# Splitting w2 for the experts: eight of them one per tile, in the order of the tile table

## What is computed

```python
    scores = jnp.einsum('bhqd,bhkd->bhqk', qh, kh) / np.sqrt(HD)
    attn = jax.nn.softmax(jnp.where(causal, scores, -jnp.inf), axis=-1)
    out = jnp.einsum('bhqk,bhkd->bhqd', attn, vh)
...
    topw, topi = jax.lax.top_k(probs, K)              # K = 4 of E = 16
    combine = jnp.sum(jax.nn.one_hot(topi, E) * topw[..., None], axis=2)
    def body(acc, expert):
        w1e, b1e, w2e, b2e, ce = expert
        hmid = jax.nn.gelu(x @ w1e + b1e, approximate=False)
        return (acc + (hmid @ w2e + b2e) * ce[:, None], None)
```

## Time and profile before

| | us |
|---|---|
| median of 3 runs | 1704.41 (1701.32 to 1704.91) |
| the profiled execution | 1689.59 |
| its span, from its first to its last instruction | 1687.9 |
| PE busy | 1591.6 (94%) |
| DVE busy | 1191.6 (71%) |
| ACT busy | 1067.2 (63%) |
| POOL busy | 510.5 (30%) |

### The profile page before, as it was taken

How to read it: one execution, slowest core, us unless ns; L and a number is a source line. 1 busy time by engine, 2 the same in 40 slices (tenths; PEclk the granted TensorE clock), 3 DMA queues, 4 the chain that set the end, 5 groups by cost and what they waited for, 6 DMA issues and landing times.

```text
span 1687.9 us, 35758 instructions
## 1 busy us (share of the span) xinstructions
PE 1591.6 (94%) x12470; PEld 1338.8 (79%) x12470; DVE 1191.6 (71%) x2754; ACT 1067.2 (63%) x2702; POOL 510.5 (30%) x430
## 2 busy tenths in 40 slices
PE   5999989999999999999999999997999999999995
PEld 4888866777677777777776776776989999999995
DVE  6988947667776777677677767678775666666662
ACT  4555547666666765676666667667755666666663
POOL 3434400000210300301202103004485555554654
PEclk9999989999999999999999999999999999999998
DMA  3122110000110100200201102045699777777773
GB/s 99 38 88 76 38 63 2 1 26 2 43 50 1 60 33 1 82 11 15 78 1 47 46 2 85 8 155 183 152 245 257 190 173 167 187 169 172 183 159 38
DMA packets 94976, 144.54 MB, mean 86 GB/s; under 512 B 12576, under 2 KB 55120, under 8 KB 94800
## 3 DMA queue, kind: packets, MB, share of 16 engines
q1 hardware_dynamic: 64448, 102.19, 19.3%
q0 software_dynamic: 28896, 38.62, 12.2%
q10 hardware_dynamic: 1456, 1.44, 0.3%
HBM read 90.76 MB, written 51.46 MB: 84 GB/s over the span
## 4 chain that ended last, share of the span: by engine, by line
PE 55%; ACT 16%; DVE 9%; issue 3%; DMA 2%; SPq 1%; POOL 0%; POOLq 0%; DVEq 0%; ACTq 0%
PE ex_H L1753 12%; PE ex_Y L1767 11%; ACT xa_prob L1336 8%; PE xa_work L1251 6%; PE xa_work L1176 6%; PE xa_S L1205 5%; PE xa_work L1187 4%; PE xa_work L1234 4%; PE xa_work L1222 4%; ACT xa_probT L1350 4%; DVE xa_nmax L1454 3%; PE ex_X L1735 2%; DVE xa_prob L1466 2%; DMA out<-ex_y,ahead_bits 1%; DVE xa_q1lo L1447 1%
## 5 line engine op out<-in xcount | busy, mean ns | idle before, releaser
L1336 ACT ACTIVATE xa_prob<-xa_S,xa_nmax 128x512 f32<-128x512 f32 (+3 forms) x512 | 265.9, 534 | 126.8 <-DVE xa_nmax L1454 126.1
L1869 POOL DMA_INDIRECT out<-ex_y,ahead_bits x158 | 259.0, 1640 | 220.0 <-POOLq L1865 92.0
L1753 PE MATMUL ex_H<-ex_xT,ex_w 128*128 128x256 f32 x1896 | 248.3, 288 | 0.1
L1767 PE MATMUL ex_Y<-experts_w_hi,ex_hT 128*128 x1264 | 238.9, 282 | 5.9 <-issue 5.9
L1753 PEld LDWEIGHTS ex_H<-ex_xT,ex_w 128*128 128x128 f32 x1896 | 234.1, 193 | 0.4 <-issue 0.3
L1767 PEld LDWEIGHTS ex_Y<-experts_w_hi,ex_hT 128*128 128x128 f32 x1264 | 200.7, 190 | 6.1 <-issue 6.1
L1454 DVE TENSOR_REDUCE xa_nmax<-xa_S 128x2 f32<-128x1024 f32 (+3 forms) x256 | 198.0, 816 | 1.2 <-PE xa_S L1210 1.2
L1622 POOL DMA_INDIRECT expert_rows<-kept_xn,kept_rows x112 | 112.4, 1004 | 274.1 <-DVE xa_prob L1466 249.3
L1350 ACT ACTIVATE xa_probT<-xa_work 128x512 f32<-128x512 f32 x256 | 139.6, 602 | 80.6 <-PE xa_work L1222 80.6
L1840 DVE TENSOR_TENSOR ex_hT<-ex_h,ex_hT 128x512 fp32r<-128x512 f32 x158 | 109.2, 693 | 107.0 <-ACT ex_hT L1792 103.3
L1767 PE MATMUL ex_Y<-experts_w_lo,ex_hT 128*128 x632 | 177.5, 281 | 0.0
(11 more groups left out here) (363 smaller groups left out, 3614.7 us busy)
## 6 DMA issues: line engine op xcount, KB each, us to landing
ex_w_raw<-in_w SPq DMA_DIRECT2D x29, 512.0 KB, 3.7
kept_x<-expert_rows SPq DMA_DIRECT2D x50, 273.0 KB, 4.5
ahead_ctx<-in_w SPq DMA_DIRECT2D x25, 512.0 KB
ahead_x<-in_w SPq DMA_DIRECT2D x25, 512.0 KB
kept_xn<-expert_rows SPq DMA_DIRECT2D x29, 273.0 KB, 4.6
experts_w_lo<-in_w SPq DMA_DIRECT2D x6, 1024.0 KB, 5.8
expert_rows<-ahead_spare SPq DMA_DIRECT2D x32, 136.5 KB
a_x<-in_x SPq DMA_DIRECT2D x8, 512.0 KB, 4.6
```

The lines of the kernel that those rows point to most:

```text
L1336: m = act.activation(prob[n % 2][:, odd, PROB_AT[i]:PROB_AT[i] + width], SB[slot[at]][:, odd, col:col + width], ACT.Exp, bias=nmax[n % 2][ ...
L1753: m = pe.matmul(bank[:, (f % 2) * ROWS:(f % 2 + 1) * ROWS], ww[:, c, f * P:(f + 1) * P], xx[:, c, :], start=(i == 0), stop=(i == len(terms ...
L1767: m = pe.matmul(bank[:, a * D:(a + 1) * D], hh[:, f, a * P:(a + 1) * P], W2[:, bass.ds(own * WE + f * D, D)], start=(i == 0), stop=(i == l ...
L1869: pool.indirect_dma_start(out, bass.IndirectOffsetOnAxis(tail[j % NT][:, a, 0:1].bitcast(I32), 0), y[j % NY][:, a, :], None, compute_op=AL ...
```

## The change

The eight experts 0, 1 and 8 to 13 are no longer split in a fixed order before tile 0's results. DVE sorts them (`order_w2`, in pair 56): those that own a tile in the first part of the table, by their number, then the others. `high_late` and `low_late` split the first of them behind the last pair and one more in each of tiles 0 to 6, at an address that ACT and DVE load from this order. `results` of tile j waits for the j-th alone (the last for all later tiles). Expert 6's halving moves ahead of the turns of pair 63.

The last batch's chain, the pads, its scatters, the store of its x2, the second part of the table and the four buffers all come three tiles later; the first part of the table holds for 27 tiles. `give_tables` comes right behind `turn_tables`, ahead of `hidden`, and both use the bank of tile 17.

In pairs 57, 59, 61 and in those with p = 4 or 7 of batches 0 to 6, turn 2 comes ahead of `soften` of block 3 in the plan, which changes ACT's order alone.

```diff
-SURE_TILES = 24
+SURE_TILES = 27
+LATE_W2, N_LATE = ((0, (0, 2)), (2, (8, 6))), 8
...
+    def order_w2(self, dve, w, done, late_w2):
+        tiles, rank, ranked = self.scr[0:1, 1, :], self.scr[0:1, 3, 0:N_LATE], self.scr[0:1, 3, N_LATE:2 * N_LATE]
+        for at, (first, n) in LATE_W2:
+            i = dve.tensor_scalar(rank[:, at:at + n], tiles[:, first:first + n], 1.0, float(2 * E), ALU.is_ge, ALU.mult)
+        i.then_inc(done.of("has"), 1)
+        w.wait_ge(done, "has")
+        dve.tensor_tensor(rank, rank, late_w2, op=ALU.subtract).then_inc(done.of("rank"), 1)
+        w.wait_ge(done, "rank")
+        dve.max(ranked, rank).then_inc(done.of("ranked"), 1)
+        w.wait_ge(done, "ranked")
+        dve.tensor_scalar(rank, ranked, float(E), float(2 * E), ALU.is_ge, ALU.mult).then_inc(done.of("had"), 1)
+        w.wait_ge(done, "had")
+        dve.tensor_tensor(self.scr_i[0:1, 0:N_LATE], rank, ranked, op=ALU.subtract).then_inc(done.of("order"), 1)
...
-TURN_AT, W2_IN_PAIR = 14, {61: (2, 3), 62: (4, 5), 63: (14, 15)}
-CHAIN = {1: [("find3", B - 1)], 2: [("norm3", B - 1)], ...
+LATE_MAX = (57, 59, 61)
+TURN_AT, W2_IN_PAIR = 17, {61: (2, 3), 62: (4, 5), 63: (14, 15)}
+CHAIN = {4: [("find3", B - 1)], 5: [("norm3", B - 1)], ...
...
-            plan += [*turns, *high_w2(6, 7), *low_w2(6, 7), *finish, *scatters]
+            plan += [*high_w2(6), *turns, *low_w2(6), *high_w2(7), *low_w2(7), *finish, *scatters]
...
+        in_front = 3 if n in LATE_MAX or coming < B and p in (4, 7) else 2
-        plan += [("scores", (n, 3)), ("scores", (n, 2)), *start, *turns[0:2], *high_w2(*one), ("soften", (n, 3)), *turns[2:4], ("soften", (n, 2))]
+        plan += [("scores", (n, 3)), ("scores", (n, 2)), *start, *turns[0:2], *high_w2(*one), *turns[2:in_front], ("soften", (n, 3)), *turns[in_front:4], ("soften", (n, 2))]
...
-    plan += [("add_b2", (b - 1, 1)), ("store_x2", b - 1), ("split_w1", 0), ("turn_x", 0), ("load_x", 2), *high_w2(8, 1, 0, 9), *low_w2(8, 1),
+    plan += [("add_b2", (b - 1, 1)), ("store_x2", b - 1), ("split_w1", 0), ("turn_x", 0), ("load_x", 2), ("high_late", 0), ("low_late", 0),
...
-        steps = [("turn_x", j + 1), ("load_x", j + 3), ("turn_tables", None), *(high_w2(10, 11, 12, 13) + low_w2(0, 9, 10) if j == 0 else []),
-                 ("hidden", j), *(low_w2(11, 12, 13) if j == 0 else []), *chain[:1], ("split_w1", j + 2), ("load_w1", j + 4), ("results", j - 1), *chain[1:]]
+        steps = [("turn_x", j + 1), ("load_x", j + 3), ("turn_tables", None), ("give_tables", None), ("hidden", j), ("high_late", j + 1), *chain[:1], ("split_w1", j + 2), ("load_w1", j + 4), ("low_late", j + 1), ("results", j - 1), *chain[1:]]
...
+            elif step == "high_late":
+                w.wait_ge(t_dve, "order")
+                w.wait_ge(s_pe, (B * PAIRS - 1, 1, 1))
+                w.wait_ge(pv_pe, (B * PAIRS - 1, 1))
+                for i, loaded in enumerate(w2_in):
+                    w.wait_ge(loaded, i)
+                mine = act.value_load(tables.scr_i[0:1, at:at + 1], min_val=0, max_val=E - 1)
+                act.activation(W2_hi[:, bass.ds(mine * WE, WE)], f32(W2_lo[:, bass.ds(mine * WE, WE)]), ACT.Copy
+                               ).then_inc(high_late.of(at), 1)
...
+            elif step == "low_late":
+                w.wait_ge(high_late, at)
+                mine = dve.value_load(tables.scr_i[0:1, at:at + 1], min_val=0, max_val=E - 1)
+                own = bass.ds(mine * WE, WE)
+                dve.tensor_tensor(W2_lo[:, own], f32(W2_lo[:, own]), f32(W2_hi[:, own]), op=ALU.subtract).then_inc(low_late.of(at), 1)
...
-FEW, MORE, MORE_AT = 2, 4, 20
-CHAIN_AT, CHAIN_END = 3, 12
+FEW, MORE, MORE_AT = 2, 4, 23
+CHAIN_AT, CHAIN_END = 6, 15
...
-                w.wait_ge(gone["low_w2"], 13)
+                w.wait_ge(gone["low_w2"], 7)
+                w.wait_ge(gone["low_late"], min(j, N_LATE - 1))
```

More of the change, by code:

```diff
@@ L144, in of_part @@
     def of_part(part):
-        return ["one", "up", "tiles_i", "tiles", *(("less",) if part else ()), "cum", "hit", "owner", "hit_tiles", "before",
+        return ["one", "up", "tiles_i", "tiles", *(("less",) if part else ()), "cum", *(() if part else ("has", "rank", "ranked", "had", "order")), "hit", "owner", "hit_tiles", "before",
                 *(("some", "first", "behind", "here", "used", "owner_some") if part else ()), "row",
@@ L170, in find_owners @@
         mult, add, sub = ALU.mult, ALU.add, ALU.subtract
-        w.wait_ge(done, "cum")
+        w.wait_ge(done, "cum" if part else "order")
         dve.tensor_scalar(hit, cum, number[:], None, ALU.is_le).then_inc(done.of("hit"), 1)
@@ L916 @@
 OF_LOAD = {e_: i for i, (first, last) in enumerate(LOAD_W2) for e_ in range(first, last)}
-TURN_AT, W2_IN_PAIR = 14, {61: (2, 3), 62: (4, 5), 63: (14, 15)}
-CHAIN = {1: [("find3", B - 1)], 2: [("norm3", B - 1)], 3: [("transpose_x3", (B - 1, c)) for c in range(KC)], 4: [("route", B - 1)],
-         5: [("choose", B - 1)], 6: [("mark", B - 1), ("weigh_gates", B - 1)], 7: [("place", B - 1)], 8: [("turn_gates", B - 1)],
-         9: [("add_b2", (B - 1, 0))], 10: [("add_b2", (B - 1, 1))]}
+LATE_MAX = (57, 59, 61)
+TURN_AT, W2_IN_PAIR = 17, {61: (2, 3), 62: (4, 5), 63: (14, 15)}
+CHAIN = {4: [("find3", B - 1)], 5: [("norm3", B - 1)], 6: [("transpose_x3", (B - 1, c)) for c in range(KC)], 7: [("route", B - 1)],
+         8: [("choose", B - 1)], 9: [("mark", B - 1), ("weigh_gates", B - 1)], 10: [("place", B - 1)], 11: [("turn_gates", B - 1)],
+         12: [("add_b2", (B - 1, 0))], 13: [("add_b2", (B - 1, 1))]}
 ALONE = [at for steps in CHAIN.values() for at in steps if at[0] in ("transpose_x3", "route", "place", "turn_gates", "add_b2")]
@@ L1033, in cross_attention @@
         tables = Tables(sb, lg)
-        sb("room_in_front_of_w2", [P, 16])
+        late_w2 = sb("room_in_front_of_w2", [P, 16])[0:1, 0:N_LATE]
         heads = ExitStack()
@@ L1087, in cross_attention @@
         low_w2 = signal("low_w2", [at for step, at in plan if step == "low_w2"])
+        high_late, low_late = signal("high_late", range(N_LATE)), signal("low_late", range(N_LATE))
         x3_pe, x3_ev = signal("x3_pe", blocks), signal("x3_ev", blocks)
@@ L1378, in scalar @@
                 end = B * PAIRS - 1
-                w.wait_ge(s_pe, (end, 1, 1), at == 0)
-                w.wait_ge(s_pe, (end - 1, 1, 1), at == 1)
                 w.wait_ge(pv_pe, (end - PAIRS // 2, 1), at in (2, 3))
-                w.wait_ge(pv_pe, (end - 1, 1), at in (6, 7, 8))
-                w.wait_ge(pv_pe, (end, 1), 9 <= at < 14)
+                w.wait_ge(pv_pe, (end - 1, 1), at in (6, 7))
                 w.wait_ge(k_pe, end, at >= 14)
@@ L1584, in vector @@
                     tables.count_tiles(dve, w, t_dve, 0, kept, count)
+                    w.wait_ge(late_set, 0)
+                    tables.order_w2(dve, w, t_dve, late_w2)
                 elif at == 1:
@@ L1595, in gpsimd @@
                 pool.memset(f32(gates[:]), 0.0).then_inc(gates_zero.of(0), 1)
+                for to, (first, n) in LATE_W2:
+                    i = pool.iota(late_w2[:, to:to + n], [[1, n]], base=first, channel_multiplier=0, allow_small_or_imprecise_dtypes=True)
+                i.then_inc(late_set.of(0), 1)
             elif step in ("find2", "find3"):
@@ L1723, in tensor @@
                 w.wait_ge(x_lo, TURN_AT)
-                tables.transpose(pe, w, t_dve, XB[0], ident).then_inc(tables_pe.of(0), 1)
+                tables.transpose(pe, w, t_dve, x_bank(TURN_AT), ident).then_inc(tables_pe.of(0), 1)
             elif step == "turn_x":
@@ L1813, in vector @@
                 w.wait_ge(tables_pe, 0)
-                tables.give_out(dve, t_dve, 1, XB[0], ahead, routing)
+                tables.give_out(dve, t_dve, 1, x_bank(TURN_AT), ahead, routing)
             elif step == "split_w1":
```

14 lines of the change are left out of this document (7 added, 7 removed).

## The result

| | before | after |
|---|---|---|
| median of 5 runs each, us | 1704.41 (1701.32 to 1706.37) | 1689.28 (1686.68 to 1693.37) |
| ratio to before, 95% interval | | 0.9918 (0.9897 to 0.9939) |
| the profiled execution / its span, us | 1689.59 / 1687.9 | 1687.96 / 1686.2 |

A forecast was written before the change was run, and what follows sets the result against it. PE was taken to bound the kernel, so only its stalls and half-clock stretches could give time. Gains 9.6 + 8.1 + 3.4 = 21.1 us took the profiled 1689.6 to 1668.5, the median 1704.4 to 1683.3; range 1675 to 1694.

The forecast's parts named there:

- Turn 2 before the exponentials: Attention, 17 pairs: ACT's earlier copy frees PE's bank; 11.4 us of waits less 0.7 left gives 10.7 gain.
- Rival A: Attention pairs give nothing: the exponentials slip by the copy and PE waits for the next bank; 1693 us, 12%.
- Ordering the experts: Pair 56: six small DVE operations behind the scan delay the low half of o; cost 1.05 us.
- One expert per tile: First results and tiles 0 to 6: stall and half clock go, 8.6 gained, 0.5 lost to DVE; net -8.1 us.
- hand-over: From attention to tile 0's first results: PE's 5.9 us stand and 2.7 of half clock behind it would go.
- Rival B: DVE binds tiles 0 to 6 through register loads or POOL's adds: 5 to 10 us lost, 1689 to 1693, 12%.
- Three tiles later: Last batch's chain, its DMAs and the table move three tiles, nothing shifting against each other; -3.4 us.
- the hand-out of the table: Second part ahead of DVE's hidden-layer work: PE's wait of 2.0 us and 1.7 of slow clock go, 3.7.
- the late rows of x: PE's waits for x, 4.2 us, expected again at X(17), X(18) and X(23), the transpositions of those tiles' x.
- Rival C: First results: a late expert's half is still PE's last wait, behind gelu and SP; 8.6 stays, 1692 us, 5%.
- D: Tiles 0 to 6: halving with an address from a register takes ACT and DVE far longer; slower, 1716 us, 4%.

The follow-up runs named there:

- a_after: Profiled rerun of the full change, unchanged, on the chip where the kernel before took 1687.75 us: 1677.67 us, span 1676.0.
- experiments 4: Kernel before plus turn 2 in front and the late experts one per tile; chain, table and deep buffers left as before: 1693.02 us, ratio 0.9934 to before.
- experiment 5: Full change without the move by three tiles, with the table handed out ahead of the hidden layer: 1685.92 us, ratio 0.9912 to before.
- 11: experiment 5 with the tail (a tile's row numbers and gates) copied later, from tile 24 on: 1688.53 us, ratio 0.9898 to before.
- experiments 2: Full change with turn 2 behind the exponentials in all pairs, as before: 1688.86 us, ratio 1.0005 to before.
- 3: Kernel before with turn 2 ahead of the exponentials in the same 17 pairs, alone: 1677.22 us, ratio 0.9938 to before.
- experiment 6: Full change with w2 in the fixed order, keeping turn 2 in front, the three-tile move and the early table: 1701.12 us, ratio 0.9982 to before.

## Why the prediction was right or wrong

*Turn 2 before the exponentials* (-10.7, with 0.7 left over): right in kind and place, too high in size. 11.4 us of waits are gone, 2.8 us of new ones stand there: 8.6. What was mis-sized is the leftover: "about 0.1 us of each such wait" is 0.3 ahead of the next projection at six of the pairs. Alone, the edit brought 10.5 us in the timed runs. Rival A (nothing) is out.

*Ordering the experts* (1.05): right in place, near in size. DVE's six operations sit between the scan at 1045.26 and the low half of o at 1046.27, and PE waits 0.8 longer for the latter.

*One expert per tile* (-8.1): right in the attention's end and in tiles 0 to 9, and this is the step that failed in the total. In a_after, where nothing else happened at the hand-over, the first results came at 1162.3, straight behind the hidden layer of tile 1, and H(0) to H(10) took 62.5 us against 70.4 to 71.3: 8 to 9, as predicted. The first results had been forecast for 1159.5, since the attention was to give 9.6; H(0) came 7.2 us sooner than in before. Of the missing 2.4 us, 2.1 is the larger leftover (2.8 and not 0.7), and 0.4 lies in PE's last wait for a copy of probT (1.3 and not 0.9), which the prediction does not have. DVE did not bind: it was busy for 53.8 of the 66.2 us from H(0) to H(10), and PE waited for no low half of w2. Rival B's mechanism showed only in experiments 4, 5 and 11, where the routing runs in the same tiles. The late subtractions had been put to a rule of the Trainium skill; here are all eight of after (ns, least, median and most):

```profile
L1581 DVE TENSOR_TENSOR experts_w_lo<-experts_w_lo,experts_w_hi x8: 1224/1226/1285, 1159.4 to 1210.9; - x8
```

They take 1224 to 1285 ns among POOL's scatter-adds, against 1209 to 1225 in the earlier trace rows. The Trainium skill (SBUF — State Buffer, "SBUF: two separate sides") says that such an operation and a GpSimd operation that reads SBUF lock each other out for a whole instruction; the most that a subtraction lost here is 76 ns. The rule may hold for other POOL work; no run here shows it.

*Three tiles later* (-3.4): the hand-out of the table is right (2.0 of stall gone; experiment 5 against 4 has 4.9 in H(10) to H(26)). The sentence that failed is "Against each other nothing moves, and SP's queue of loads between them is the same; so I expect the late rows of x again, 4.2 us". The order was the same, but the time between was not: the tiles ahead had become quicker, by the 5.9 and 2.0 us of stall and the slow clock behind each. In the full change the late rows cost 4.3 to 7.6 us (after: 7.4, and 1.1 for x2's addition) where the old kernel pays 3.7 to 4.7. Behind that, POOL's adds lag in tiles 30 to 40: up to 30.6 us in the full change and 25.8 in before, with up to 7.3 us of PE lost. The worst share of the DMA engines did not rise (1.06 in both). And the new cut of the table put the longest run of adds that wait for one another at other tiles. That the stalls had been time in which POOL and the DMA engines caught up is how I read this; it is argued, since every edit that removed a stall changed other things too. "Nothing moves" was judged by queue and not by what each queue must carry in the time that is left.

Of the Trainium skill (DMA: Bandwidth & Descriptors, "Specifications"), one figure bears on this: a limit of about 358 GB/s from HBM for a core. Here the engines were busy all the time at 287 GB/s, and elsewhere, at a share of 1.08, they moved 340. The bytes per second alone would not have told that they were full; the share did, but it did not tell whether PE had to wait.

*The sum.* Terms of 21.1 us; measured 14 and 16 where before takes 1703 to 1706, and about 10 where it takes 1688 (one run of the full change, 10.1 below before's median; experiments 2 and 3 add up to 0 + 10.5). The forecast and its range held the first, with the largest term nearly right. Of the second, 11.5 us of hand-over and table, nothing arrived on the quicker chip. On the other, 14 to 16 less the 10.5 of turn 2 leaves 4 to 6; but turn 2 was measured alone on the quicker chip only, and against experiment 6 one expert per tile is worth 13, so there the share of each part stays open.

That 1683.3 came near is in part luck. The 14.8 us between profile and median were carried over from before to after, but the profiled execution of after lay 1.3 us below its median. The profile of before, 1689.6, has the time that this kernel takes on the quicker chip, and the marks of that chip's traces (see the last section). So the 14.8 are most likely the distance between two chips, and the terms were read on one kind and the median taken on the other. On the kind from which the rows come the change gives about half of the 21.1.

*Rival C* is out (the 5.9 us are gone), *D* too: the copy with an address from a register takes 1.06 us on ACT, the subtraction 1.22, as with a fixed one.

## What to carry to other kernels

A stall on the engine that sets the end is also slack for everything that runs behind it. Before counting it as gain, look at the stretch after it: where a queue of dependent scatter-adds is already far behind its tile, or rows already land late, the time can come back there. And check that a profile and the timed runs beside it are of one kind before carrying their difference over. A lag with a limit (here five tiles' buffers, 27 us) is worth a row of its own in the forecast: before stood at 25.8, 1 us below it.

## What the runs showed of the hardware

**PE's signals come late, on one kind of chip.** In after, DVE and ACT both wait at the hand-over for signals of PE, whose matmuls had ended some 3 us before by the profile's modelled ends. `remote` means that the profile could not match the signal to its sender. The timelines of DVE and ACT:

```profile
1165.27 0.69 DVE L1500 TENSOR_TENSOR xa_x<-xa_work,xa_x 128x512 f32<-128x512 f32 x1 [3.39 <-remote]
...
1165.26 0.60 ACT L1813 ACTIVATE ex_xT<-ex_X 128x512 fp32r<-128x512 f32 x1 [6.45 <-remote]
```

This is the 3.26 us ahead of the hidden layer of tile 1. Something alike happens once in each of the batches 2 to 7. Timeline of PE and DVE of after, in the first pair of the third batch:

```profile
457.51 0.26 PE L1228 MATMUL xa_S<-ahead_bits 64*128 64x128 bf16 x4
...
457.34 0.75 DVE L1471 SCALAR_TENSOR_TENSOR xa_q1lo<-xa_work,ahead_bqT,xa_q1hi 128x512 fp32r<-128x512 f32 x1 [0.51 <-issue]
459.38 1.02 DVE L1478 TENSOR_REDUCE xa_nmax<-xa_S 128x2 f32<-128x512 f32 x2 [1.29 <-remote]
```

The scores were done at 457.77; the reduction that reads them started at 459.38. The trace has PE's signal for them at 459.36, 1.6 us after the last matmul's modelled end; in a_after the signal comes at 460.32 and that end is 460.30. In a_after the same reduction starts as soon as DVE is free, 0.2 us after the scores:

```profile
460.02 0.28 PE L1228 MATMUL xa_S<-ahead_bits 64*128 64x128 bf16 x4
...
460.52 1.01 DVE L1478 TENSOR_REDUCE xa_nmax<-xa_S 128x2 f32<-128x512 f32 x2
```

All nine traces of kernels with turn 2 in front that were taken on the chips where before takes 1703 to 1706 have these six waits (6.5 to 7.3 us in all), and most of them take 1 to 5 us longer from H(0) to H(2); the two on the other chip have neither. It eats most of the attention's gain in those traces, and yet the timed ratio there is the better one.

The trace of before is of the other kind in every respect. It has no wait that ends by `remote` ahead of the tiles, like the four from the first chip; the nine have 5 to 7 each on DVE. It holds 14588 semaphore updates, the four 14579 to 14607, the nine 11990 to 12487. And its 1689.59 us lies among the 17 timed runs of before on the first chip (1684.11 to 1692.10) and below all 34 on the other (1698.52 to 1712.35). So it was most likely taken on a chip of the first kind, while its timed runs, 1701 to 1706, are like those of the second. The record does not name the chip. There is then no trace of before from the slower kind; whether its timed runs there lose more by late signals stays open, and with it why the change gives 14 to 16 us there and 10 here. The nine traces hold fewer semaphore updates, so who ended a wait is less sure in them.

**One place, three outcomes.** The kernels that are the full change from H(0) on ran through tiles 26 to 42 in 98.2, 98.2, 100.0 and 105.5 us in four executions, with a lag of 26.0, 27.1, 27.1 and 30.6 us at the worst tile. Small differences in the scatter-adds, near the limit of the lag, become microseconds. One trace of such a kernel does not tell what a change is worth.
